# GpSimd adds up the probabilities before one product with ones; key weights move into the squaring; five probability slots

## What is computed

```python
# layer 1, "squared"
q, k, v = (ln(x) @ W.T for W in (Wq, Wk, Wv))            # split into 16 heads
q, k = head_norm(q * gamma + beta) * D**-0.5, head_norm(k * gamma + beta)
attn = where(causal, (q @ k.T) ** 2, 0)
o = (attn @ v) / (attn.sum(-1) + EPS)
x = x + o @ Wo.T
# layers 2 and 4, "gated": one key and value head per token, picked by a gate
x = x + softmax(causal(q @ k_shared.T / sqrt(D))) @ v_shared
# layer 3, "mqa": one key and value head for all query heads, biases, output projection
x = x + softmax(causal(q @ k.T / sqrt(D))) @ v @ out_w.T + out_b
```

## Time and profile before

| what | value |
|---|---|
| median of 3 runs | 4797.77 us (4794.02 to 4806.56) |
| profiled execution | 4810.55 us |
| its span | 4808.8 us, 76616 instructions |
| TensorE matmuls | 4292.6 us, 89% |
| VectorE | 1770.6 us, 37% |
| ScalarE | 1546.9 us, 32% |
| GpSimd | 847.3 us, 18% |
| mean granted clock of TensorE | 0.961 |

### The profile page before, as it was taken

The page is one execution under the profiler, slowest core; times in us unless marked ns, Lnnn a source line. Parts: engine busy times, 40 slices in busy tenths (PEclk is TensorE's granted clock), DMA queues, the critical chain, the costliest instruction groups (busy, mean ns, idle before and its releaser), DMA issues.

```text
span 4808.8 us, 76616 instructions
## 1 busy us (share of the span) xinstructions
PE 4292.6 (89%) x32674; PEld 1781.0 (37%) x32674; DVE 1770.6 (37%) x2666; ACT 1546.9 (32%) x1985; POOL 847.3 (18%) x1495
## 2 busy tenths in 40 slices
PE   6899999996999898898898989989899897988987
PEld 4343434333333333333333333333333333333333
DVE  1222212122544444434444443443443444444342
ACT  1433333340223323323333333332222233232333
POOL 1311212121101211202112221211112012011012
PEclk8999999998999999999999999999999999999999
DMA  1001010003000100101001010000001001010010
GB/s 62 18 1 36 18 36 18 18 18 102 18 1 1 54 1 23 32 1 38 16 23 32 12 43 1 25 30 26 28 1 46 9 1 54 1 37 17 1 36 27
DMA packets 63405, 115.67 MB, mean 24 GB/s; under 512 B 8672, under 2 KB 9184, under 8 KB 63072
## 3 DMA queue, kind: packets, MB, share of 16 engines
q1 hardware_dynamic: 63072, 110.77, 7.2%
HBM read 77.19 MB, written 33.55 MB: 23 GB/s over the span
## 4 chain that ended last, share of the span: by engine, by line
PE 58%; DVE 6%; issue 5%; ACT 3%; DMA 2%; POOL 2%; POOLq 0%; SPq 0%; DVEq 0%; ACTq 0%
PE banks L1085 14%; PE banks L1043 10%; PE banks L995 9%; PE banks L1027 8%; PE banks L988 7%; DVE maxima_soft L811 5%; PE banks L1024 3%; ACT probs_soft L732 3%; PE banks L1052 2%; PE banks L1184 2%; DMA tiles_soft<-out 1%; PE banks L1159 1%; PE banks L1094 1%; POOL tiles_soft L637 0%; POOL rest_soft L705 0%
## 5 line engine op out<-in xcount | busy, mean ns | idle before, releaser
L811 DVE TENSOR_REDUCE maxima_soft<-banks 128x2 f32<-128x1024 f32 (+3 forms) x1152 | 1036.6, 953 | 1309.8 <-PE banks L1052 828.6
L732 ACT ACTIVATE probs_soft<-banks 128x1024 f32<-128x1024 f32 (+1 forms) x960 | 848.5, 936 | 1252.4 <-PE banks L1027 1250.2
L1043 PE MATMUL banks<-k_soft,q_soft 32*128 32x512 f32 (+3 forms) x4608 | 547.0, 544 | 69.6 <-ACT probs_soft L732 67.6
L646 POOL TENSOR_SCALAR_AFFINE_SELECT probs_soft<-probs_soft 128x512 f32<-128x512 f32 x384 | 239.2, 635 | 1963.5 <-ACT probs_soft L732 1961.8
L1027 PE MATMUL banks<-q_soft,k_soft 32*128 32x512 f32 (+3 forms) x4608 | 487.1, 505 | 0.0
L1085 PE MATMUL banks<-probs_soft,v_soft 128*32 128x512 f32 (+3 forms) x4608 | 435.6, 497 | 13.4 <-ACT shift_soft L718 9.5
L1085 PE MATMUL banks<-probs_soft,ones 128*32 128x512 f32 (+3 forms) x4608 | 433.5, 495 | 0.0
L732 ACT ACTIVATE probs_squared<-banks 128x1024 f32<-128x1024 f32 (+1 forms) x320 | 282.8, 936 | 387.7 <-PE banks L1027 387.6
L1043 PEld LDWEIGHTS banks<-k_soft,q_soft 32*128 32x128 f32 x4608 | 187.1, 186 | 320.1 <-issue 302.3
L1024 PE MATMUL banks<-shift_soft,ones 32*128 32x512 bf16 (+3 forms) x2304 | 202.3, 339 | 113.9 <-DVE maxima_soft L811 100.9
L995 PE MATMUL banks<-g_wv,xnT_soft 128*128 128x512 f32 x512 | 251.4, 625 | 27.4 <-DVE inverse_soft L917 21.2
(11 more groups left out here) (151 smaller groups left out, 4218.7 us busy)
## 6 DMA issues: line engine op xcount, KB each, us to landing
tiles_soft<-out SPq DMA_DIRECT2D x96, 256.0 KB, 2.9
rest_soft<-out SPq DMA_DIRECT2D x96, 256.0 KB, 3.0
out<-rest_soft SPq DMA_DIRECT2D x96, 256.0 KB, 2.0
tiles_squared<-in_x SPq DMA_DIRECT2D x32, 256.0 KB, 2.9
rest_squared<-in_x SPq DMA_DIRECT2D x32, 256.0 KB, 2.9
out<-rest_squared SPq DMA_DIRECT2D x32, 256.0 KB, 2.0
raw_wq<-in_squared_wq SPq DMA_DIRECT2D x1, 1024.0 KB, 6.2
raw_wk<-in_squared_wk SPq DMA_DIRECT2D x1, 1024.0 KB, 8.5
```

Source lines behind the costliest of these rows:

```text
L646: ins = pool.affine_select(out=cells, in_=cells, compare_op=ALU.is_ge, fill=0.0, base=0, pattern=[[0, HG], [1, P]], channel_multiplier=-1)
L732: act.activation(slot(ph, n)[:, 2 * a:2 * a + 2, 0:width], score_pair(e, a)[:, :, 0:width], ACT.Exp if soft else ACT.Square, scale=SCALE). ...
L811: ins = dve.reduce_max(m["maxima"][:, ph % 2, 2 * a:2 * a + 2, t, p], score_pair(e, a)[:, :, col:col + P * blocks], AX_X)
L1043: ins = pe.matmul(psum[:, score_bank(e, i), col:col + P * blocks], m["q"][D * i:D * i + D, ph % NG, P * t:P * t + P], k_of(ph)[D * i:D * i ...
```

## The change

- `sm` is one unit for each chunk of 512 queries: one product of ones with `added`, a tensor [128, 2 chunks, 4 heads, 512] in SBUF, 512 columns for each of four heads. The products over all key blocks are gone, and so is VectorE's addition of part C into the sums.
- `added` is filled by GpSimd in eight events `add` per phase: masked probabilities of the key blocks are added block by block in float32. `add` n stands at half 2n+3, the last one at half 1 of the next phase. The sum of chunk 0 stands at half 12, that of chunk 1 at half 6 of the next phase.
- In the squared act `key_weight`, `vscale` and the scaled values go. VectorE writes D x (variance + EPS), GpSimd raises it to the power -0.5 (`kvar`), and ScalarE uses the result as the scale of the squaring. That scale is one number for each key and head, so a squaring works on one head and one key block at a time: 48 instructions a phase where there were 20.
- The ring of probabilities has five slots. A slot is free when its `av` and its `add` are done.
- `logit_parts` and `v_parts` share one buffer. `WEIGHT` of `sm` goes from 3.2 to 1.1, and `sm` isn't halved any more.

```diff
-SLOTS = 6
+SLOTS = 5
+ADDS = {1: [(384, 128, 384)], 2: [(0, 256, 256)], 4: [], 5: [(0, 512, 0)], 6: [(0, 512, 0)], 7: [(0, 512, 0)],
+        8: [(0, 384, 128), (384, 128, 384)], 9: [(0, 256, 256)]}
+ADD_AFTER = {n: sum(o < n for o in ADDS) + 1 for n in ADDS}
+ADD_AFTER.update({0: ADD_AFTER[1], 3: ADD_AFTER[4]})
+CHUNK_ADDS = (2, len(ADDS))
+SUMS_AT = (12, 6)
@@ phase
+    for n in ADDS:
+        if n < NKB - 1:
+            at[2 * n + 3].append(("add", ph, n))
+    if ph:
+        at[1].append(("add", ph - 1, NKB - 1))
@@
-        at[h + 2].append(("more", ("sm", of, part)))
-        at[h + 3].append(("sm", of, part))
...
+        at[SUMS_AT[c]].append(("sm", of, c))
+        for event, later in sums_done(kinds[of // NG], of, c):
+            at[SUMS_AT[c] + later].append(event)
@@ wait_slot
-            wait_work(eng, ("sm", old[0], KEY_BURSTS[old[1]][1]))
+            wait_work(eng, ("av", old[0], KEY_BURSTS[old[1]][1]))
+            eng.wait_ge(sg.probs_added, len(ADDS) * old[0] + ADD_AFTER[old[1]])
@@ gpsimd
+                elif u == "add":
+                    _, ph, n = e
+                    c, part, parts = KEY_BURSTS[n]
+                    pool.wait_ge(sg.probs_ready, 2 * (of_kind["keys", ph, n] + 1))
+                    pool.wait_ge(sg.probs_masked, masks_until(ph, part, n))
+                    total = m["added"][:, c]
+                    if n in (1, 4):
+                        if ph:
+                            wait_work(pool, ("sm", ph - 1, c))
+                        if n == 1:
+                            pool.tensor_copy(total[:, :, 0:P], slot(ph, 0)[:, :, 0:P])
+                            ins = pool.tensor_tensor(total[:, :, P:CHUNK], slot(ph, 0)[:, :, P:CHUNK], slot(ph, 1)[:, :, 0:CHUNK - P], ALU.add)
+                        else:
+                            ins = pool.tensor_tensor(total, slot(ph, 3), slot(ph, 4), ALU.add)
+                    else:
+                        pool.wait_ge(sg.probs_added, len(ADDS) * ph + ADD_AFTER[n] - 1)
+                    for x, (col, width, q0) in enumerate(ADDS[n]):
+                        if x or n == 1:
+                            then(ins)
+                        sums = total[:, :, q0:q0 + width]
+                        ins = pool.tensor_tensor(sums, sums, slot(ph, n)[:, :, col:col + width], ALU.add)
+                    ins.then_inc(sg.probs_added, 1)
...
+                elif u == "kvar":
+                    _, ph, c = e
+                    wait_free(pool, e)
+                    if ph >= NG:
+                        pool.wait_ge(sg.probs_ready, 2 * (of_kind["keys", ph - NG, NKB - 1] + 1))
+                    pool.tensor_tensor(m["key_scale"][:, ph % NG, TPC * c:TPC * c + TPC, :].rearrange("p t i -> p (t i)"),
+                                       m["key_var"][:, c].rearrange("p t i -> p (t i)"), k["minus_half"][:], ALU.pow)\
+                        .then_inc(sg.key_scales, 1)
@@ scalar, keys
+                    if not soft and n == 0:
+                        act.wait_ge(sg.key_scales, NC * (ph + 1))
...
+                            for kb, _, cols, col in parts:
+                                for x in range(2):
+                                    i = 2 * a + x
+                                    ins = act.activation(slot(ph, n)[:, i, col:col + cols], score_pair(e, a)[:, x, col:col + cols],
+                                                         ACT.Square, scale=m["key_scale"][:, ph % NG, kb, i:i + 1])
@@ tensor
+                elif u == "sm":
+                    _, ph, c = e
+                    out = free(e)
+                    if not soft:
+                        pe.wait_ge(sg.query_squares, place["qsq", ph, c] + 1)
+                        pe.matmul(out, k["head_eps"][:].rearrange("p i d -> p (i d)"), m["query_square"][:, c], start=True, stop=True)
+                    pe.wait_ge(sg.probs_added, len(ADDS) * ph + CHUNK_ADDS[c])
+                    for i in range(HG):
+                        ins = pe.matmul(out[D * i:D * i + D, :], k["ones"][:], m["added"][:, c, i, :], start=soft, stop=True,
+                                        skip_group_check=not soft)
+                    ready(e, ins)
```

More of the change, by code:

```diff
@@ L95, in features @@
 def features(ph):
-    return [(u, ph, c) for c in range(NC) for u in ("q2", "k2", "ksq")] + [("kvar", ph, c) for c in range(NC)] + [("vscale", ph)]
+    return [(u, ph, c) for c in range(NC) for u in ("q2", "k2", "ksq")] + [("kvar", ph, c) for c in range(NC)]
 def keys_and_values(kind, s):
@@ L165, in phase @@
         at[h + 1].append(("av", of, part))
-        at[h + 2].append(("more", ("sm", of, part)))
-        at[h + 3].append(("sm", of, part))
-        if part != "B":
-            for event, later in sums_done(kinds[of // NG], of, 0 if part == "A" else 1):
-                at[h + 3 + later].append(event)
+    for c in range(NC):
+        of = ph - c
+        if of < 0:
+            continue
+        at[SUMS_AT[c]].append(("sm", of, c))
+        for event, later in sums_done(kinds[of // NG], of, c):
+            at[SUMS_AT[c] + later].append(event)
     return at
@@ L255, in plan @@
     last = NG * stages - 1
-    events += [("av", last, "C"), ("sm", last, "C")] + [e for e, _ in sums_done(kinds[-1], last, 1)]
+    events += [("add", last, NKB - 1), ("av", last, "C"), ("sm", last, 1)] + [e for e, _ in sums_done(kinds[-1], last, 1)]
     events += [("rload", stages - 1, t) for t in range(TILES)]
@@ L519, in act_program @@
     order = {name: [e for e in events if e[0] == name] for name in
-             ("load", "rload", "stats", "out", "mxr", "krep", "vst", "ksq", "qsq", "kvar", "vscale", "nrm", "rs", "rw", "gate")}
+             ("load", "rload", "stats", "out", "mxr", "krep", "vst", "ksq", "qsq", "kvar", "nrm", "rs", "rw", "gate")}
     order["picks"] = [e for e in events if e[0] in ("kall", "vall")]
@@ L573, in rows_of, with masks_until @@
         return dram[stages[s][1], P * t:P * t + P, :]
-    def masks_until(ph, part):
-        return 6 * ph + (6 if part == "C" else 3)
+    def masks_until(ph, part, n=None):
+        masked = [o for o, burst in enumerate(KEY_BURSTS) if burst[1] != "B"]
+        last = n if n is not None else parts_of(part)[0][-1]
+        return len(masked) * ph + sum(o <= last for o in masked)
     def earlier(name, e, *kind):
@@ L887, in _ @@
                     wait_work(dve, e)
[L888 to L897 removed]
+                    if place[e] >= NC:
+                        dve.wait_ge(sg.key_scales, place[e] - NC + 1)
+                    dve.tensor_scalar(m["key_var"][:, c], work[:, bank(e), 0:HG * TPC].rearrange("p (t i) -> p t i", i=HG), EPS, float(D),
+                                      ALU.add, ALU.mult).then_inc(sg.work_free[bank(e)], 1)
+                elif u == "av" and e[2] == "C":
                     _, ph, part = e
[L899 to L900 removed]
+                    out = y_of(ph)[:, CHUNK:T]
+                    wait_free(dve, ("av", ph, "B"))
                     wait_work(dve, e)
@@ L905, in _ @@
                     part = "AC"[c]
-                    wait_free(dve, ("sm", ph, part))
+                    wait_free(dve, ("sm", ph, c))
                     wait_free(dve, ("av", ph, part))
@@ L1064, in _ @@
                         pe.wait_ge(sg.probs_masked, masks_until(ph, part))
-                    if u == "av" and g == 0 and soft:
+                    if g == 0 and soft:
                         if kind_of(s) == "gated":
@@ L1070, in _ @@
                     if not soft:
-                        pe.wait_ge(sg.values_scaled, ph + 1)
-                        c = "ABB".index(part) if part != "C" else 1
-                        if u == "sm" and part != "C" and fresh:
-                            pe.wait_ge(sg.query_squares, place["qsq", ph, c] + 1)
-                            pe.matmul(out, k["head_eps"][:].rearrange("p i d -> p (i d)"), m["query_square"][:, c],
-                                      start=True, stop=True)
+                        for n in range(NT // 2):
+                            need(("v2", s, g // 2, n))
                     for x, (kb, q0, width, n, col) in share(products, e, opening):
                         for i in range(HG):
-                            if u == "sm":
-                                left = k["ones"][:] if soft else m["key_weight"][:, ph % NG, kb, i:i + 1].broadcast_to([P, D])
-                            elif soft:
+                            if soft:
                                 left = m["v"][:, s % 2, kb, :]
@@ L1085, in _ @@
                             ins = pe.matmul(out[D * i:D * i + D, q0:q0 + width], left, slot(ph, n)[:, i, col:col + width],
-                                            start=(x == 0 and (soft or u == "av" or part == "C")),
-                                            stop=(x == len(products) - 1 or not soft), skip_group_check=not soft)
+                                            start=(x == 0), stop=(x == len(products) - 1 or not soft), skip_group_check=not soft)
                     ready(e, ins)
```

58 lines of the change are left out of this document (19 added, 39 removed).

## The result

The changed kernel took 4787.9 us (median; 4776.5 to 4798.0), the kernel before 4797.9 on the same chips. The ratio is 0.9977, 95% interval 0.9968 to 0.9986. The forecast was -64 us; -10 us came. That is 0.23%, less than the 0.3% that I called a measurement's limit. With 14 runs of each kernel the sign is clear of the noise, and the size lies between -7 and -15 us.

A forecast was written before the change was run, and what follows sets the result against it. TensorE, busy 4292.6 of 4808.8 us, was taken as the bound, with the drain of score banks in halves without filler. 4808.8 - 235 + 58 - 77 + 12 + 138 + 40 = 4745, -64; from median 4797.8: 4734 us, range 4520 to 4910.

The forecast's parts named there:

- the floor of a half: Half of a phase without filler: the burst waits until the previous burst's first score banks are drained, 2.52 us.
- light phase: Soft phase whose work list is blocked or empty: 2 of 9.0 us of removed sums show, 14 such phases, 28 us.
- I am wrong if: Tests: light phases 5 us or more shorter, TensorE's GpSimd waits under 200 or over 500 us, ScalarE waiting for `probs` slots.
- -202: Whole kernel: the forecast of -64 us without the +138 us of waits behind GpSimd's additions.
- GpSimd's additions, +138 forecast: GpSimd's queue: additions delay `stats` (+80), `out` (+35), `ksq` (+20) and the last phase (+3); bounds 40 and 330 us.
- upper bound: Highest figure for waits behind GpSimd's additions, 330 us, including 1 us a phase for late masks (60).
- The clock, +40 forecast: Light soft phases: halves stripped of sums leave longer gaps, some three more clock drops in 14 phases, +40 us (0 to 135).
- The power, 0 forecast: GpSimd in the squared act: two small powers a phase, given no term of their own in the sum.
- The end, +3 forecast: Last phase: it ends on `add 9` instead of two products, +3 us.
- -77: TensorE in squared phases: 80% of 136.7 us of sums shows, -109, new sums +32; bounds -105 and -40 us.
- The rival in which GpSimd's order sets the pace: Additions ahead of `stats`, `out` and `ksq` cost TensorE 330 us instead of 138: 4926 us (4812 to 5050), chance 0.25.
- The rival of the clock: Most bare halves run at the lower clock level, 135 us instead of 40: 4812 to 4870 us, chance 0.07.

The follow-up runs named there:

- the additions made short: The changed kernel with every GpSimd addition and copy cut to 4 columns of each head, order and waits kept: 4613.0 us, ratio 0.9609.
- the squaring alone: The kernel before with key weights applied in the squaring and `vscale` gone, sums still on TensorE, six slots: 4817.7 us, ratio 1.0034.

## Why the prediction was right and wrong

**What held.** The sums on TensorE were mostly covered by the floor of a half: with the additions made short, taking 442 us of net work off it brought 189 us, forecast 202. The prices of a full addition, of the squaring, of GpSimd's total (2989.6 us, forecast 2.9 ms) and the idle time of TensorE (821 us, forecast some 850) held. The light phase of the earlier trace rows went from 55.6 to 53.4 us (others of its kind are longer, up to 60.7 us at a clock of 0.78), and the slots were not waited for. The products with `ones` took 144.9 us (110.4 + 34.5), forecast 128: 112 of the 128 groups ran at full clock and took 1.07 us, the others 1.1 to 1.9 us at a mean clock of 0.92 and less. The stretch of the earlier trace rows by which I reckoned 5.8 us for a squared burst holds 15 phases and not 16, so it is 6.2 us; no term changes by that. No test of "I am wrong if" came out: the waits for GpSimd are 333 us, and light phases are within 5 us of what they were.

**What failed is the clock's part in the price of the additions.** The forecast was -202 + 138 = -64; measured is -189 + 177, about -11. So 13 us were lost in the first part and 39 in the second.
- **GpSimd's additions, +138 forecast, +177 measured.** I had added up waits and nothing else, and as waits the sum was right: 144 us of idle time of TensorE (120 for GpSimd, 24 for VectorE behind it). Part of that is luck, because two misses cancel. With against without full additions, the waits for `tiles` are 47 us longer, where I had taken 80 for `ln`; those for `key_square` 25 (forecast 20); those for VectorE's `scaled_out` and `picking` 27 (forecast 35 for `out`); and those for late masks, which I had only in the upper bound, 43 us, up to 12.0 us at once. Of the wait for `tiles`, about 23 us came by SyncE's queue, which I had looked past when I listed who is queued behind. What the term lacked altogether is that TensorE also runs slower with the full additions: 32 us more for the same 27554 matmuls, at a clock of 0.925 instead of 0.942.
- **The clock, +40 forecast.** I had counted three drops in 14 light phases, bare halves only, at about 1 us each, and had put the clock around the waits for GpSimd at nothing, without a reason. That is the step that failed. The price came from two bursts of the same matmuls: the one at 1988.24 took 1.04 us at a granted clock of 1.00, the one at 1993.45 took 1.94 at 0.50. The three drops a phase were an estimate; no run shows the term of 40 us by itself, and what the runs show in its place is time at the lower level. The traces have 372 us there before, 531 with the additions short and 716 after. The first 159 us are the part that I had priced: at 0.23 to 0.3 us each an estimated 37 to 48 us, as forecast. The other 185 us come with the additions, and they are the 32 us above.
- **The power, 0 forecast, 14 to 25 us measured** (the squared act of the trace, and the whole kernel). "Two small powers a phase" was priced by the row of another small operation (228 ns for 16 elements). The trace of before had a power that warned, 549 ns for a single number per partition:

```profile
L635 POOL TENSOR_TENSOR rstd_soft<-var_eps_soft,minus_half 128x1 f32<-128x1 f32 x96 | 52.7, 549 | 102.8 <-DVE var_eps_soft L831 101.9
```

  Its price was measured beside full additions. Beside the short ones, where it would be a part of the -189, it wasn't; in the kernel before it can be at most the 16 us of the squaring alone. So it may account for the 13 us of the first part, which isn't shown.
- **The end, +3 forecast, +15 measured** (75.8 against 60.8 us). The last additions come one behind another, and nothing lies beside them. With the additions short the last phase takes 58.8 us:

```profile
4548.40:4607.20 58.80, 33.44 (x332) 14.30 (x330) 7.59 (x13) 20.92 (x26) 17.74 (x31) 0.82 0.18 55
```

  The full ones therefore cost 17 us there, of which 12 are idle time of TensorE (most of it a mask that comes late behind them) and 5 slower matmuls (38.16 against 33.44 us).

By acts, the forecast for the squared one comes to about -31 us (-77, +12, +20 for `ksq` and +14 for three `ln` clusters), and the spans show +2. There the additions cost 59 us of the 176 (1194 us without them, 1253 with them), where I had 34. In the soft act they cost 117, where I had 104.

The rival in which GpSimd's order sets the pace named the right mechanism; it asked for 216 us of such waits and got 172 (333 - 161). The rival of the clock (most bare halves at the lower level, 135 us instead of 40, 4812 to 4870) was right in kind and was given 0.07: by itself it was too small to turn the sign, but together with the first it took nearly all of the gain.

**VectorE beside GpSimd's additions.** VectorE's product of `y` with the reciprocals went from 692 ns to 1529 (above). Five of the 32 take 4.27 to 4.72 us, each with an addition of 4.50 to 4.52 us beside it. With the additions cut short it is back near its old price:

```profile
L955 DVE TENSOR_TENSOR y_squared<-y_squared,sums_squared 128x512 f32<-128x512 f32 x32 | 22.7, 709 | 1.1
```

while the maxima, which read PSUM, stayed at 1220 ns (1221 before). The product cost 27 us more of VectorE (48.9 against 22.1), and no wait of TensorE names that product. What I hadn't priced is the soft act: four small instructions of the gate between SBUF tensors went the same way, `logits` from 298 ns with the additions short to 1905, and with them `is_max` from 260 to 1196. They cost 29 us of VectorE; whether any of it reached TensorE wasn't tried. The traces give the times; what holds VectorE up beside an addition they don't show.

**Open.** Whether filled gaps would speed up the kernel before wasn't tried, and no experiment changed the clock alone. The prices of 0.23 and 0.3 us for a microsecond at the lower clock are one experiment and two pairs of phases; between whole kernels the figure runs from 0.17 to 0.43, so what is worked out from them is an estimate. Phases with the same work differ by up to 5 us from one kernel to the next at another clock (60.7 us at 0.78, 55.9 at 0.90), so a gain of 10 us can't be put down to one cause by the median alone.

## What to carry to other kernels

Work that is taken off the bounding engine comes back only where that engine was the last to arrive: read the floor of a step first, then count how much of the removed work stood above it (here 442 us of work gave 189 us, additions short). When work moves to an engine with a queue, follow the queue through every engine that waits on it, the DMA-issuing one too: a store that waits for a late result holds up loads that don't need it (about 23 us here). And price pauses of TensorE twice, as the wait and as the slower clock that goes with it (144 us and 32 us here); where a pause can't be removed, filling it can be worth more than leaving it (26 us here, for 54 us of useless work).

## What the runs showed of the hardware that I had not expected

- A power on GpSimd takes 2918 ns for 16 numbers per partition, a product of the same shape 221.
- 54 us of useless matmuls made a kernel 26 us faster; the mean granted clock rose from 0.930 to 0.942.
- Shortening VectorE's row maxima, and with them TensorE's waits for them (167.8 to 36.8 us), took 88 us off the busy time of the same 27554 matmuls (3930.3 to 3842.6 us).
- Beside GpSimd's additions, VectorE's small instructions between SBUF tensors took up to 6.4 times as long (298 ns with the additions short, 1905 with full ones).
